# Scores of one tile of keys as two products a head, and several pieces of work moved earlier or later, in a macaron block on one core

## The chip, the cores and the metric

One NeuronCore of a Trainium2 chip runs the whole program. The metric is the device time of one execution in microseconds (us). Engines: TensorE (PE, with its weight loads PEld), VectorE (DVE), ScalarE (ACT), GpSimd (POOL) and SyncE (SP), which issues the DMAs.

## The reference

The block is half a feed-forward, attention, half a feed-forward, each with a layer norm ahead and a residual, on `x` of 2 x 512 rows and width 512. All is in fp32.

```python
x = x + 0.5 * ffn(layernorm(x))        # silu(a) * b @ down; a, b from scaled weights, 1792 wide
x = x + attn(layernorm(x))
x = x + 0.5 * ffn(layernorm(x))

# attn: 32 heads of 128 in 8 groups of G = 4 that share a key and a value head
q, k = rmsnorm(x @ Wq.T), rmsnorm(x @ Wk.T);  v = x @ Wv.T
scores = q @ k.T / sqrt(128)
bias = where(key > query, -1e30, slope[head] * (key - query))
out = softmax(scores + bias) @ v @ Wo.T
```

## The kernel before, in words

Every fp32 product is three products of split operands: a value is an upper part `_h` and a rest `_l` (the value less the upper part), and `matmul3` (lines 345 to 347) adds h*h, h*l and l*h in one PSUM bank. ScalarE makes most upper parts by a cast, VectorE or GpSimd the rests by a subtraction.

The feed-forward runs in steps of two chunks of the inner width, each with seven products in place of eight on mixed (added or subtracted) operands. In the first step `mix_lo(p, at)` (L1228 to L1235) makes the rests of the mixed tokens on VectorE, 1024 columns each.

The attention has 64 units n = 8 g + 4 b + t: group g of four heads, batch b, tile t of 128 queries. The attention is causal, so a unit with t has t + 1 tiles of 128 keys; t = 0 has one. The units are software-pipelined: the program is written out by hand for each engine as slots n = 0 to 63, and in slot n TensorE does

1. `scores(n)` (L574): per head three products of (t + 1) x 128 columns into a bank of its own, from `qT_h`, `qT_l` and `kT_h`, `kT_l`;
2. the values of unit n - 1 (`weigh_values`, L604 to L609, from `probT_h` and `probT_l`);
3. two of the seven products of a pair of projections of unit n + 4 (LEAD = 4; from group 2 on);
4. `turn_rows(n + 1)` (L565): transposes of the normalised rows of q and k;
5. `project_out(n - 1)`: four heads, each three products of 512 columns from `o_h`, `o_l` (the output weights) and `oT_h`, `oT_l`;
6. one or two more products of the seven, and the transposes of unit n's probabilities (L590).

Results go to eight PSUM banks. `result` takes the bank that was taken longest ago, and has TensorE wait (`evac`) until its last result was read. So an engine that reads a bank late holds up whatever takes that bank next.

VectorE in slot n: per head one custom operation (L1375) adds the bias to the scores and finds the maximum; then the inverse of the sums, `oT_l`, in even slots the sums of squares, `pair_roots(n + 2)` (L1348) and `add_products` (L1403 and L1411, which adds a product in PSUM to `rows`), then `turn_rows(n + 1)` (`qT_l`, `kT_l`, L1362 and L1367), the output's addition to `x_ring` (L1401) and `probT_l` (L1386). The roots of two units are `inverse_root` (L1090): eleven small steps on 10 columns, each waits for the one before; from the third on they read `row_root_y` and `row_root_a` or `row_root_b` from SBUF.

GpSimd in slot n (L1653): the squares of rows (L1645), `norm_rows(n + 2)` (L1651, waits for the roots), the rests of values, and per group of heads the rests of the next weights: `split_o` (`o_l`, four chunks of 512, in the second slot of a group) and `split_qkv` (`ahead_l` and `w_l_late`, 768 columns each; `QKV_WHEN` names the slots). ScalarE makes their upper parts and signals each.

Between the first feed-forward and the attention, `from_ffn_to_attention` does the projections of the first four units, `turn_normed` (transposes of normalised tokens) and `turn_rows(0)`.

Of the kernel before, what the change touches and what calls it, by code (L numbers as in the profile page):

```python
# [10 lines left out]
ALU = mybir.AluOpType  # L11
ACT = mybir.ActivationFunctionType
# [72 lines left out]
def build(nc, scaled, x_between, x, ffn_w, ffn_fac, ffn_fix, factor_lo, w_qkv, w_o, norm_w, out):  # L85
# [3 lines left out]
    with ExitStack() as ctx:  # L89
        def sb(name, shape, dt=F32, stack=ctx):  # L90
            return stack.enter_context(nc.sbuf_tensor(name, [P, *shape], dt))
# [112 lines left out]
        v_h, v_l = sb("v_h", [B, TB, HD], F32R), sb("v_l", [B, TB, HD], F32R)  # L204
        kT_h, kT_l = sb("kT_h", [S], F32R), sb("kT_l", [S], F32R)
        qT_h, qT_l = sb("qT_h", [G, P], F32R), sb("qT_l", [G, P], F32R)
# [100 lines left out]
        def qkv_place(g, block):  # L307
            at = QKV_BLOCKS[g][block]
            return qkv_h[at], qkv_l[at]

        def paired(n):
# [17 lines left out]
        def tensor_program():  # L329
# [184 lines left out]
            def from_ffn_to_attention():  # L514
                gate_up(0, STEPS - 1, 0, 1, (1,))
                gate_up(0, STEPS - 1, 1, 1)
                turn_normed(1, 0)
                down(0, STEPS - 1, 1)
                for n in range(LEAD):
                    project(n, "left")  # L520
                    project(n, "right")
                    if n == 1:
                        turn_normed(1, 1, (0, 1))
                turn_rows(0)
                turn_normed(1, 1, (2, 3))

# [47 lines left out]
            def scores(n):  # L574
                keys = (unit(n)[2] + 1) * P
                turned_q, turned_k = results["turn_q", n], results["turn_k", n]
                pe.wait_ge(evac[turned_q.bank], turned_q.nth)
                pe.wait_ge(evac[turned_k.bank], turned_k.nth)
                for h in range(G):
# [110 lines left out]
        def scalar_program():  # L690
# [187 lines left out]
            def from_ffn_to_attention():  # L878
                turn_normed(1, 0)
                for n in range(LEAD):  # L880
                    project_left(n)
                    project_right(n)
                    if n == 1:
                        turn_normed(1, 1, (0, 1))
                turn_rows(0)
                turn_normed(1, 1, (2, 3))

# [76 lines left out]
            def exponentials(n, heads):  # L964
                keys = (unit(n)[2] + 1) * P
                for h in heads:
                    r = results["scores", n, h]
                    act.wait_ge(evac[r.bank], r.nth)
# [42 lines left out]
            def slot(n):  # L1011
# [7 lines left out]
                if n:  # L1019
                    weigh_values(n - 1)  # L1020
                exponentials(n, range(soon, G))
                probabilities(n)
                ahead = n + LEAD
                if ahead < FIRST_PAIRED:
                    project_left(ahead)
                elif ahead < UNITS:
                    take_sum(ahead, 1) if n % 2 == 0 else take_sum(ahead - 1, 7)
                turn_rows(n + 1)
                if n % 2 == 0 and paired(n + 2):
# [49 lines left out]
        def vector_program():  # L1079
# [157 lines left out]
            def ffn_first(p):  # L1237
# [76 lines left out]
            def from_ffn_to_attention():  # L1314
# [14 lines left out]
                values_lo(2)  # L1329
                sum_squares(2)  # L1330
                values_lo(3)
# [3 lines left out]
                turn_normed(1, 1, (2, 3))  # L1335

# [32 lines left out]
            def scores(n):  # L1369
                g, _, i = unit(n)  # L1370
                keys = (i + 1) * P
                for h in range(G):
                    r = results["scores", n, h]
# [79 lines left out]
            def slot(n):  # L1453
# [21 lines left out]
                turn_rows(n + 1)  # L1475
                if ahead < FIRST_PAIRED:
# [41 lines left out]
        def pool_program():  # L1518
# [134 lines left out]
            def slot(n):  # L1653
                g, at = divmod(n, B * TB)
                if at == 1:
                    split_o(g, range(G))
                ahead = n + LEAD
                if n % 2 == 0 and paired(n + 2):
                    square_rows(n + 2)
                    square_rows(n + 3)  # L1660
                mixes_now = QKV_MIX_WHEN.get(at, ()) if SEVEN_FROM <= g + 1 < HKV else ()
                if at == 4:
                    mix_qkv(g + 1, *mixes_now)
                if n + 2 < UNITS:
                    norm_rows(n + 2)
# [8 lines left out]
                if at == 3:  # L1674
                    mix_qkv(g + 1, *mixes_now)
                if g < HKV - 1:
                    split_qkv(g + 1, *QKV_WHEN[g + 1 >= SEVEN_FROM].get(at, ()))
                if 0 <= n - LEAD - 1 < PAIRS:
# [288 lines left out]
```

## Time and profile before

| | us |
|---|---|
| median of 3 runs (lowest, highest) | 1238.32 (1237.34, 1238.6) |
| profiled execution | 1237.32 |
| its span | 1236.0 |
| granted TensorE clock | 1.00 |
| PE busy | 1215.9 (98%) |
| DVE busy | 827.4 (67%) |
| ACT busy | 756.6 (61%) |
| POOL busy | 649.1 (53%) |

The span is the time between the first and the last instruction of the profiled execution; what lies around it is 1.3 us. PE is the fullest engine by far. The duration of a matmul in the records is longer than the distance to the next one, since matmuls are pipelined: read starts, not durations, for what one costs. An instruction's idle time before it and what ended it stand in brackets behind its row.

### The profile page before, as it was taken

The page shows a single profiled execution, that of the slowest core. Times are in us where ns is not written, and L with a number is a line of the kernel's source. Part 1 is how long each engine was busy: PE and PEld are TensorE (multiplying, and loading weights), DVE is VectorE, ACT ScalarE, POOL GpSimd, SP SyncE. Part 2 cuts the span into 40 slices and gives each one's busy share as a digit, 9 for nine tenths or more (in the row PEclk, how much of TensorE's full clock was granted, in tenths as well). Part 3 has the DMA queues.
Part 4 walks back from the last instruction along what each step waited for, and adds up shares of the span by engine and source line. Part 5 has one row for each costly group of instructions (what it writes and reads, how often), then busy time and mean ns, then how long its engine had stood idle before and what let it go on. Part 6 is the DMA issues. An engine that isn't in the chain of part 4 may idle for free.

```text
span 1236.0 us, 18593 instructions
## 1 busy us (share of the span) xinstructions
PE 1215.9 (98%) x6418; PEld 1065.9 (86%) x6418; DVE 827.4 (67%) x2002; ACT 756.6 (61%) x1760; POOL 649.1 (53%) x526
## 2 busy tenths in 40 slices
PE   6999999999999999999999999999999999999999
PEld 5788888899998999999999999999999888888887
DVE  7966666676666667667677677667767778655555
ACT  4554442347677767767767767767767764544442
POOL 4696661734676624724824823823824343765550
PEclk9999999999999999999999999999999999999999
DMA  6142322212112122122122122122122010221101
GB/s 232 40 157 106 106 104 102 86 52 85 54 67 103 37 84 94 43 86 94 44 86 86 52 86 86 52 80 93 52 77 86 26 53 17 69 69 52 52 17 68
DMA packets 33453, 93.77 MB, mean 76 GB/s; under 512 B 4113, under 2 KB 4785, under 8 KB 31313
## 3 DMA queue, kind: packets, MB, share of 16 engines
q1 hardware_dynamic: 33120, 92.29, 21.8%
q8 instruction: 52, 0.85, 0.3%
q14 instruction: 41, 0.33, 0.1%
q10 hardware_dynamic: 240, 0.30, 0.1%
HBM read 62.69 MB, written 29.88 MB: 75 GB/s over the span
## 4 chain that ended last, share of the span: by engine, by line
PE 91%; DVE 4%; ACT 2%; POOL 1%; issue 1%; DMA 1%; SPq 0%; DVEq 0%; ACTq 0%; POOLq 0%
PE bank L345 21%; PE bank L347 21%; PE bank L346 21%; PE bank L590 5%; PE bank L424 4%; PE bank L430 4%; PE bank L425 4%; PE bank L604 3%; PE bank L609 3%; PE bank L605 3%; PE bank L569 2%; PE bank L373 1%; DVE stats L1106 1%; PE bank L572 1%; PE bank L361 0%
## 5 line engine op out<-in xcount | busy, mean ns | idle before, releaser
L1651 POOL TENSOR_TENSOR rows<-rows,row_root_y 128x640 f32<-128x640 f32 x64 | 80.6, 1260 | 205.1 <-DVE row_root_y L1102 205.1
L970 ACT ACTIVATE prob<-prob,neg_top 128x128 f32<-128x128 f32 (+3 forms) x256 | 141.2, 553 | 77.0 <-DVE neg_top L1375 76.4
L1645 POOL TENSOR_TENSOR square<-rows 128x640 f32<-128x640 f32 x64 | 79.2, 1254 | 161.0 <-DVE rows L1411 125.1
L1520 POOL TENSOR_TENSOR w_l_late<-raw_late,w_h_late 128x512 fp32r<-128x512 f32 (+1 forms) x59 | 90.5, 1548 | 74.9 <-ACT w_h_late L727 74.9
L979 ACT ACTIVATE prob<-prob,inverse 128x128 f32<-128x128 f32 (+3 forms) x256 | 123.0, 553 | 4.6 <-DVE inverse L1380 4.6
L1386 DVE TENSOR_TENSOR probT_l<-bank,probT_h 128x512 fp32r<-128x512 f32 x160 | 101.4, 683 | 21.8 <-ACT probT_h L985 21.7
L985 ACT CAST probT_h<-bank 128x512 fp32r<-128x512 f32 x160 | 84.6, 596 | 41.9 <-PE bank L590 41.9
L1375 DVE CUSTOM_DVE_ANT_0 prob<-bank,bias 128x128 f32<-128x128 f32 (+3 forms) x256 | 109.7, 484 | 0.0
L1168 DVE SCALAR_TENSOR_TENSOR x_rows<-bank,x_rows 128x512 f32<-128x512 f32 x112 | 75.7, 687 | 45.9 <-PE bank L430 45.9
L345 PE MATMUL bank<-o_h,oT_h 128*128 128x512 f32 x256 | 104.7, 409 | 0.0
L347 PE MATMUL bank<-o_h,oT_l 128*128 128x512 f32 x256 | 100.8, 394 | 0.0
L346 PE MATMUL bank<-o_l,oT_h 128*128 128x512 f32 x256 | 99.8, 390 | 0.0
L1411 DVE TENSOR_TENSOR rows<-bank,rows 128x384 f32<-128x384 f32 x72 | 40.0, 555 | 80.7 <-ACT rows L934 51.3
L345 PE MATMUL bank<-kT_h,qT_h 128*128 128x128 f32 (+3 forms) x256 | 86.5, 338 | 2.9 <-DVE qT_l L1362 2.9
L590 PE MATMUL bank<-ident,prob 128*128 128x128 f32 x640 | 81.4, 273 | 1.1 <-ACT prob L979 0.9
L347 PE MATMUL bank<-kT_h,qT_l 128*128 128x128 f32 (+3 forms) x256 | 82.2, 321 | 0.0
L346 PE MATMUL bank<-kT_l,qT_h 128*128 128x128 f32 (+3 forms) x256 | 82.1, 321 | 0.0
L590 PEld LDWEIGHTS bank<-ident,prob 128*128 128x128 f32 x640 | 73.8, 140 | 6.2 <-issue 1.7
L1520 POOL TENSOR_TENSOR w_l_early<-raw_early,w_h_early 128x512 fp32r<-128x512 f32 x37 | 49.6, 1357 | 41.9 <-ACT w_h_early L727 41.9
L1392 DVE TENSOR_TENSOR oT_l<-bank,oT_h 128x512 fp32r<-128x512 f32 x64 | 44.2, 690 | 30.9 <-ACT oT_h L990 30.9
L604 PE MATMUL bank<-probT_h,v_h 128*128 128x512 f32 x160 | 63.9, 399 | 0.3 <-ACT probT_h L985 0.3
L605 PE MATMUL bank<-probT_h,v_l 128*128 128x512 f32 x160 | 62.8, 392 | 0.0
(213 smaller groups left out, 3747.8 us busy)
## 6 DMA issues: line engine op xcount, KB each, us to landing
x_ring<-x_between SPq DMA_DIRECT2D x64, 256.0 KB, 2.6
x_between<-x_ring SPq DMA_DIRECT2D x56, 256.0 KB, 2.0
raw_late<-w_qkv SPq DMA_DIRECT2D x8, 1536.0 KB, 6.5
raw_early<-ffn_w SPq DMA_DIRECT2D x21, 512.0 KB, 4.0
scaled<-raw_early SPq DMA_DIRECT2D x21, 512.0 KB, 2.7
raw_late<-scaled SPq DMA_DIRECT2D x21, 512.0 KB, 3.7
raw_late<-w_o SPq DMA_DIRECT2D x8, 1024.0 KB, 5.0
x_between<-x_rows SPq DMA_DIRECT2D x8, 256.0 KB, 2.0
```

The source lines that it names most:

```text
L345: pe.matmul(bank, lh, rh, start=first, stop=False, skip_group_check=more)
L346: pe.matmul(bank, lh, rl, start=False, stop=False, skip_group_check=more)
L347: return pe.matmul(bank, ll, rh, start=False, stop=last, skip_group_check=more)
L590: last = pe.transpose(bank[:, h * P:(h + 1) * P], prob[:, h, j * P:(j + 1) * P], ident[:, :])
L604: pe.matmul(bank[:, :], v_h[:, b, j, :], turned[2 * j], start=j == 0, stop=False)
L605: pe.matmul(bank[:, :], v_l[:, b, j, :], turned[2 * j], start=False, stop=False)
L970: last = act.activation(p, p, ACT.Exp, bias=neg_top[:, h:h + 1], scale=-1.0, accum_out=total[:, h:h + 1])
L979: act.activation(p, p, ACT.Copy, scale=inverse[:, h:h + 1]).then_inc(prob_done, 1)
L985: act.copy(probT_h[:, j, :, :], banks[r.bank][:, :].rearrange("p (h q) -> p h q", h=G)).then_inc(probT_hi_done, 1)
L1375: dve.tensor_tensor_reduce(prob[:, h, 0:keys], banks[r.bank][:, 0:keys], bias[:, h, S - keys:S], -(2.0 ** -g), -MASKED, ALU.add, ALU.min, ...
L1386: dve.tensor_tensor(probT_l[:, j, :, :], banks[r.bank][:, :].rearrange("p (h q) -> p h q", h=G), probT_h[:, j, :, :].bitcast(F32), ALU.sub ...
L1520: return pool.tensor_tensor(lo, raw, hi.bitcast(F32), ALU.subtract)
```

## The change

It has six parts.

1. `in_halves(n)`: for the units with one tile of keys and n + 4 < 64 (n = 0, 4, ..., 56; fifteen of the sixteen) `kT_h` and `kT_l` lie side by side in one tile `kT`. Per head one product `qT_h` x [`kT_h` | `kT_l`] of 256 columns and one `qT_l` x `kT_h` of 128 stand in place of three of 128. Two heads share a bank. VectorE reads the second halves with two additions (rest + bias), waits for them, and then adds and reduces per head.
2. In those slots VectorE does `turn_rows(n + 1)` ahead of `pair_roots` and `add_products`.
3. GpSimd makes `o_l`'s first chunk in the first slot of a group of heads, ahead of `norm_rows`, and in the fifth slot the first block of `split_qkv` ahead of `norm_rows`.
4. `mix_lo(p, 2)` and `mix_lo(p, 3)` go from the end of `ffn_first` to `ffn_second`, one ahead of `down(p, 0, 1)` and one behind it.
5. The last `turn_normed` and `turn_rows(0)` stand ahead of the right half of project(3) on TensorE and ScalarE, and ahead of two later pieces on VectorE; in slot 0 ScalarE does `turn_rows(1)` ahead of the probabilities.
6. A dummy exponential in the transition and a dummy Silu ahead of the last values load ScalarE's tables earlier.

```diff
+        kT = sb("kT", [2, S], F32R)
+        kT_h, kT_l = kT[:, 0, :], kT[:, 1, :]
+        def in_halves(n):
+            return unit(n)[2] == 0 and n + LEAD < UNITS
@@ TensorE, from_ffn_to_attention (ScalarE alike)
                 for n in range(LEAD):
                     project(n, "left")
+                    if n == LEAD - 1:
+                        turn_normed(1, 1, (2, 3))
+                        turn_rows(0)
                     project(n, "right")
@@ TensorE, scores
+                if in_halves(n):
+                    for h in range(0, G, 2):
+                        r, bank = result("scores", n, h)
+                        for head in (h, h + 1):
+                            cols = (head - h) * 2 * P
+                            pe.matmul(bank[:, cols:cols + 2 * P], qT_h[:, head, :], kT[:, :, 0:P], start=True, stop=False, ...
+                            last = pe.matmul(bank[:, cols:cols + P], qT_l[:, head, :], kT_h[:, 0:P], start=False, stop=True, ...
+                        last.then_inc(full[r.bank], 1)
+                    return
@@ ScalarE
+                act.activation(total[:, 0:1], ident[:, 0:1], ACT.Exp)
...
+                if n == 0:
+                    turn_rows(n + 1)
                 probabilities(n)
...
+            act.activation(total[:, 0:1], ident[:, 0:1], ACT.Silu)
             weigh_values(UNITS - 1)
@@ VectorE
-                mix_lo(p, 2, 3)
...
                 product_lo(p, 1, 0, 0)
+                mix_lo(p, 2)
                 down(p, 0, 1)
+                mix_lo(p, 3)
@@ VectorE, scores
+                if in_halves(n):
+                    two = [results["scores", n, h] for h in range(0, G, 2)]
+                    for h, r in zip(range(0, G, 2), two):
+                        dve.wait_ge(full[r.bank], r.nth)
+                        rests = banks[r.bank][:, :].rearrange("p (h m c) -> p h m c", h=2, m=2)[:, :, 1, :]
+                        own_step(dve.tensor_tensor(prob[:, h:h + 2, 0:P], rests, bias[:, h:h + 2, S - P:S], ALU.add))
+                    for h in range(G):
+                        r = two[h // 2]
+                        if h == 0:
+                            own_wait()
+                        last = dve.tensor_tensor_reduce(prob[:, h, 0:P], banks[r.bank][...], prob[:, h, 0:P], ...)
+                        if h % 2:
+                            last.then_inc(evac[r.bank], 1)
+                    return
@@ VectorE, slot
-                if n % 2 == 0:
+                if in_halves(n):
+                    turn_rows(n + 1)
+                if n % 2 == 0 and n + LEAD - 2 < UNITS:
                     pair_roots(n + LEAD - 2)
                 if paired(ahead):
                     add_products(ahead, 2) if n % 2 == 0 else add_products(ahead - 1, 5)
-                turn_rows(n + 1)
+                if n + 1 < UNITS and not in_halves(n):
+                    turn_rows(n + 1)
@@ GpSimd, slot
                 if at == 1:
-                    split_o(g, range(G))
+                    split_o(g, range(1, G))
...
                 if at == 4:
                     mix_qkv(g + 1, *mixes_now)
+                    split_qkv(g + 1, *splits[:1])
+                    splits = splits[1:]
+                if at == 0:
+                    split_o(g, (0,))
                 if n + 2 < UNITS:
                     norm_rows(n + 2)
```

VectorE in a slot with one tile of keys (the same rows in each of them from the third on). `qT_l`, `kT_l` are the rests of the next unit's turned queries and keys, `row_root_*` the steps of the roots, `rows<-bank,rows` is `add_products`. Before:

```order
L1346 TENSOR_REDUCE sums<-square 128x5 x2
L1093 TENSOR_SCALAR row_root_m<-sums 128x10
L1095 TENSOR_SCALAR row_root_y<-row_root_m 128x10
L1098 SCALAR_TENSOR_TENSOR row_root_a<-row_root_y 128x10
...
L1102 SCALAR_TENSOR_TENSOR row_root_y<-row_root_b,row_root_y 128x10
L1411 TENSOR_TENSOR rows<-bank,rows 128x384
L1362 SCALAR_TENSOR_TENSOR qT_l<-bank,q_scale,qT_h 128x512
L1367 TENSOR_TENSOR kT_l<-bank,kT_h 128x128
```

and now (`kT` is both halves of the keys):

```order
L1376 TENSOR_REDUCE sums<-square 128x5 x2
L1392 SCALAR_TENSOR_TENSOR qT_l<-bank,q_scale,qT_h 128x512
L1397 TENSOR_TENSOR kT<-bank,kT 128x128
L1122 TENSOR_SCALAR row_root_m<-sums 128x10
L1124 TENSOR_SCALAR row_root_y<-row_root_m 128x10
L1127 SCALAR_TENSOR_TENSOR row_root_a<-row_root_y 128x10
...
L1131 SCALAR_TENSOR_TENSOR row_root_y<-row_root_b,row_root_y 128x10
L1456 TENSOR_TENSOR rows<-bank,rows 128x384
```

The two rests went from behind the eleven steps and the sum to ahead of them.

GpSimd in the fifth slot of a group, as it is in n = 20, 28, ..., 52. `ahead_l<-raw_late` is the moved rest, `rows<-rows,row_root_y` is `norm_rows`. Before:

```order
L1645 TENSOR_TENSOR square<-rows 128x640 x2
L1595 TENSOR_TENSOR xn<-raw_late,xn 128x768
L1651 TENSOR_TENSOR rows<-rows,row_root_y 128x640
L1520 TENSOR_TENSOR v_l<-rows,v_h 128x128 x2
L1520 TENSOR_TENSOR ahead_l<-raw_late,ahead_h 128x768
L1520 TENSOR_TENSOR ahead_l<-xn,ahead_h 128x768
```

and now:

```order
L1694 TENSOR_TENSOR square<-rows 128x640 x2
L1644 TENSOR_TENSOR xn<-raw_late,xn 128x768
L1569 TENSOR_TENSOR ahead_l<-raw_late,ahead_h 128x768
L1700 TENSOR_TENSOR rows<-rows,row_root_y 128x640
L1569 TENSOR_TENSOR v_l<-rows,v_h 128x128 x2
L1569 TENSOR_TENSOR ahead_l<-xn,ahead_h 128x768
```

The first rest stands ahead of the operation that waits for the roots, and no longer behind it.

TensorE in the change: product 2 of the unit ahead in slot 28, and the scores of unit 29 later in the same slot, with the semaphores that they wait for (`evac6` is the release of bank 6):

```order
L351 MATMUL bank<-w_h_late,xnT_hi 128x384 [waits evac6,qkv_lo]
L352 MATMUL bank<-w_l_late,xnT_hi 128x384
...
L351 MATMUL bank<-kT,qT_h 128x256 [waits evac4,evac2,evac7]
L352 MATMUL bank<-kT,qT_h 128x256
L353 MATMUL bank<-kT,qT_l 128x256
L351 MATMUL bank<-kT,qT_h 128x256 [waits evac1]
...
L351 MATMUL bank<-kT,qT_h 128x256 [waits evac6]
```

The third head of the scores takes the bank of product 2, which `add_products` of this slot reads.

## Rows read from the trace of the kernel before

**Rows 1.** The page: busy time by engine, and the chain's shares by engine.

```profile
PE 1215.9 (98%) x6418; PEld 1065.9 (86%) x6418; DVE 827.4 (67%) x2002; ACT 756.6 (61%) x1760; POOL 649.1 (53%) x526
...
PE 91%; DVE 4%; ACT 2%; POOL 1%; issue 1%; DMA 1%; SPq 0%; DVEq 0%; ACTq 0%; POOLq 0%
```

**Rows 2.** Waits of PE by releaser: us in total, times, longest us.

```profile
PE bank L345 <- DVE qT_l L1362: 2.9, 4, 1.0
...
PE bank L424 <- DVE silu L1185: 0.8, 1, 0.8
```

**Rows 3.** Timeline of PE, scores(28): start us, us, line, operation, tiles.

```profile
599.35 0.30 PE L345 MATMUL bank<-kT_h,qT_h 128*128 128x128 f32 x1
...
600.73 0.44 PE L604 MATMUL bank<-probT_h,v_h 128*128 128x512 f32 x1
```

**Rows 4.** Timeline of PE, scores(29).

```profile
610.38 0.36 PE L345 MATMUL bank<-kT_h,qT_h 128*128 128x256 f32 x1
...
611.17 0.28 PE L345 MATMUL bank<-kT_h,qT_h 128*128 128x256 f32 x1
...
611.89 0.40 PE L604 MATMUL bank<-probT_h,v_h 128*128 128x512 f32 x1
```

**Rows 5.** Timeline of DVE, slot 28.

```profile
606.53 0.17 DVE L1093 TENSOR_SCALAR row_root_m<-sums 128x10 f32<-128x10 f32 x1
...
608.67 0.55 DVE L1411 TENSOR_TENSOR rows<-bank,rows 128x384 f32<-128x384 f32 x1
609.14 0.74 DVE L1362 SCALAR_TENSOR_TENSOR qT_l<-bank,q_scale,qT_h 128x512 fp32r<-128x512 f32 x1
609.80 0.28 DVE L1367 TENSOR_TENSOR kT_l<-bank,kT_h 128x128 fp32r<-128x128 f32 x1
...
611.89 0.41 DVE L1375 CUSTOM_DVE_ANT_0 prob<-bank,bias 128x256 f32<-128x256 f32 x1
```

**Rows 6.** Timeline of ACT, slot 28.

```profile
606.29 0.69 ACT L958 ACTIVATE qT_h<-bank,q_scale 128x512 fp32r<-128x512 f32 x1 [0.43 <-PE bank L569]
...
607.41 0.84 ACT L899 CAST ahead_h<-raw_late 128x768 fp32r<-128x768 f32 x1
```

**Rows 7.** Timeline of POOL, slot 28.

```profile
608.84 1.26 POOL L1651 TENSOR_TENSOR rows<-rows,row_root_y 128x640 f32<-128x640 f32 x1 [4.76 <-DVE row_root_y L1102]
...
610.89 1.85 POOL L1520 TENSOR_TENSOR ahead_l<-raw_late,ahead_h 128x768 fp32r<-128x768 f32 x1
```

**Rows 8.** Timeline of DVE, slot 12.

```profile
416.96 1.01 DVE L1093 TENSOR_SCALAR row_root_m<-sums 128x10 f32<-128x10 f32 x1
```

**Rows 9.** Timeline of POOL, slot 12.

```profile
416.09 1.84 POOL L1520 TENSOR_TENSOR ahead_l<-xn,ahead_h 128x768 fp32r<-128x768 f32 x1
```

**Rows 10.** Timeline of DVE, the roots of the layer norm ahead of the attention.

```profile
253.64 1.12 DVE L1098 SCALAR_TENSOR_TENSOR ln_root_a<-ln_root_y 128x4 f32<-128x4 f32 x1
```

**Rows 11.** Timeline of POOL, the same moment.

```profile
253.49 1.25 POOL L1645 TENSOR_TENSOR square<-rows 128x640 f32<-128x640 f32 x1 [10.23 <-ACT rows L925]
```

**Rows 12.** Timeline of POOL, slots 8 and 9.

```profile
372.75 2.40 POOL L1520 TENSOR_TENSOR sum_l<-sum,sum_h 128x1024 fp32r<-128x1024 f32 x1
375.11 5.06 POOL L1520 TENSOR_TENSOR o_l<-raw_late,o_h 128x512 fp32r<-128x512 f32 x4
```

**Rows 13.** Timeline of ACT, slot 24, the first of a group of heads.

```profile
562.37 1.14 ACT L912 CAST o_h<-raw_late 128x512 fp32r<-128x512 f32 x2 [1.69 <-PE bank L347]
```

**Rows 14.** Timeline of PE, the third head of scores(25).

```profile
564.33 0.28 PE L345 MATMUL bank<-kT_h,qT_h 128*128 128x256 f32 x1
```

**Rows 15.** Timeline of ACT, slot 8.

```profile
373.92 1.14 ACT L912 CAST o_h<-raw_late 128x512 fp32r<-128x512 f32 x2 [1.34 <-PE bank L347]
```

**Rows 16.** Timeline of PE, the first head of project_out(8).

```profile
381.41 0.39 PE L345 MATMUL bank<-o_h,oT_h 128*128 128x512 f32 x1
```

**Rows 17.** Timeline of DVE, first feed-forward, second step's start.

```profile
50.72 5.23 DVE L1235 TENSOR_TENSOR mix_l<-mix,mix_h 128x1024 fp32r<-128x1024 f32 x2
```

**Rows 18.** Timeline of ACT, the evacuation behind the weights' splits.

```profile
64.98 1.20 ACT L759 COPY part<-bank 128x512 f32<-128x512 f32 x2
```

More of the change, by code:

```diff
@@ L204, in build @@
         v_h, v_l = sb("v_h", [B, TB, HD], F32R), sb("v_l", [B, TB, HD], F32R)
-        kT_h, kT_l = sb("kT_h", [S], F32R), sb("kT_l", [S], F32R)
+        kT = sb("kT", [2, S], F32R)
+        kT_h, kT_l = kT[:, 0, :], kT[:, 1, :]
         qT_h, qT_l = sb("qT_h", [G, P], F32R), sb("qT_l", [G, P], F32R)
@@ L523, in from_ffn_to_attention @@
                         turn_normed(1, 1, (0, 1))
-                turn_rows(0)
-                turn_normed(1, 1, (2, 3))
             def project(n, part):
@@ L578, in scores @@
                 pe.wait_ge(evac[turned_k.bank], turned_k.nth)
+                if in_halves(n):
[3 more added lines that the diff above has]
+                            cols = (head - h) * 2 * P
+                            pe.matmul(bank[:, cols:cols + 2 * P], qT_h[:, head, :], kT[:, :, 0:P], start=True, stop=False,
+                                      skip_group_check=True)
+                            last = pe.matmul(bank[:, cols:cols + P], qT_l[:, head, :], kT_h[:, 0:P], start=False, stop=True,
+                                             skip_group_check=True)
+                        last.then_inc(full[r.bank], 1)
+                    return
                 for h in range(G):
@@ L879, in from_ffn_to_attention @@
                 turn_normed(1, 0)
+                act.activation(total[:, 0:1], ident[:, 0:1], ACT.Exp)
                 for n in range(LEAD):
                     project_left(n)
+                    if n == LEAD - 1:
+                        turn_normed(1, 1, (2, 3))
+                        turn_rows(0)
                     project_right(n)
@@ L884, in from_ffn_to_attention @@
                         turn_normed(1, 1, (0, 1))
-                turn_rows(0)
-                turn_normed(1, 1, (2, 3))
             def split_qkv(g, *blocks):
@@ L966, in exponentials @@
                 for h in heads:
-                    r = results["scores", n, h]
+                    r = results["scores", n, h - h % 2 if in_halves(n) else h]
                     act.wait_ge(evac[r.bank], r.nth)
@@ L1027, in slot @@
                     take_sum(ahead, 1) if n % 2 == 0 else take_sum(ahead - 1, 7)
-                turn_rows(n + 1)
+                if n:
+                    turn_rows(n + 1)
                 if n % 2 == 0 and paired(n + 2):
@@ L1329, in from_ffn_to_attention @@
                 values_lo(2)
-                sum_squares(2)
-                values_lo(3)
+                turn_normed(1, 1, (2, 3))
                 dve.wait_ge(q_scale_done, 1 + HKV)
@@ L1334, in from_ffn_to_attention @@
                 turn_rows(0)
-                turn_normed(1, 1, (2, 3))
+                sum_squares(2)
+                values_lo(3)
             def values_lo(n):
@@ L1371, in scores @@
                 keys = (i + 1) * P
+                if in_halves(n):
[8 more added lines that the diff above has]
+                            own_wait()
+                        last = dve.tensor_tensor_reduce(prob[:, h, 0:P], banks[r.bank][:, h % 2 * 2 * P:h % 2 * 2 * P + P],
+                                                        prob[:, h, 0:P], -(2.0 ** -g), -MASKED, ALU.add, ALU.min, neg_top[:, h:h + 1])
+                        if h % 2:
+                            last.then_inc(evac[r.bank], 1)
+                    return
                 for h in range(G):
@@ L1474, in slot @@
                     add_products(ahead, 2) if n % 2 == 0 else add_products(ahead - 1, 5)
-                turn_rows(n + 1)
+                if n + 1 < UNITS and not in_halves(n):
+                    turn_rows(n + 1)
                 if ahead < FIRST_PAIRED:
@@ L1661, in slot @@
                 mixes_now = QKV_MIX_WHEN.get(at, ()) if SEVEN_FROM <= g + 1 < HKV else ()
+                splits = QKV_WHEN[g + 1 >= SEVEN_FROM].get(at, ()) if g < HKV - 1 else ()
                 if at == 4:
                     mix_qkv(g + 1, *mixes_now)
+                    split_qkv(g + 1, *splits[:1])
+                    splits = splits[1:]
+                if at == 0:
+                    split_o(g, (0,))
                 if n + 2 < UNITS:
@@ L1675, in slot @@
                     mix_qkv(g + 1, *mixes_now)
-                if g < HKV - 1:
-                    split_qkv(g + 1, *QKV_WHEN[g + 1 >= SEVEN_FROM].get(at, ()))
+                split_qkv(g + 1, *splits)
                 if 0 <= n - LEAD - 1 < PAIRS:
```

## Prediction

> **What bounds the kernel now.** I read the page first. The reader is to see that TensorE is busy 98% of the span and owns 91% of the chain that ended last [rows 1]. So only two things move the time: what TensorE issues, and where it waits. The waits by releaser come next. Inside the attention they are small: four waits for `qT_l`, 2.9 us together and 1.0 the longest, and one of 0.8 for a `silu` in the first half [rows 2]. There is little left to win by taking waits away, and every new wait of TensorE counts in full. The timelines of one unit and its neighbours then give durations, and, on VectorE and GpSimd, how much room each result has before TensorE asks for it. Times are in microseconds of the profiled run.
>
> **1. The scores of one tile of keys, 15 units (n = 0, 4, ..., 56).** Now twelve products of 128 columns go from 599.35 to the next line at 600.73: 1.38 for twelve, 0.115 each [rows 3]. Twelve of 256 columns go from 610.38 to 611.89: 1.51, and 0.12 each after the first of a stretch [rows 4]. The changed unit has four of 256 and four of 128 columns: 4 x 0.12 + 4 x 0.115 = 0.94. It saves 1.38 - 0.94 = 0.44, I take 0.43. Fifteen units would give 6.4; the first is counted under 4, so here 14 x 0.43 = -6.0. Width costs almost nothing between 128 and 256 columns, and that is all the gain. Bounds: 0.115 less if a 256-wide pair hides as well as a 128-wide one (-7.6), and 0.06 more for each if changing widths costs something (-2.7).
>
> The Trainium skill ("TensorE: Matmul & The Clock Gate", Back-to-back issue gap) gives for one isolated product a gap that grows with its columns over 2.4 GHz. By that rule 256 + 128 columns cost what 3 x 128 do, and this term would be about zero. The rows show otherwise (0.115 against 0.12), so the sum keeps -6.0.
>
> **2. VectorE and ScalarE in such a slot.** VectorE has two operations of 256 elements more; a 256-wide one holds it 0.41, paced 0.34 [rows 5], and the exponentials start up to 1.0 later. ScalarE still waits 0.43 for TensorE before `qT_h` at 606.29 [rows 6], so the delay ends there. Cost 0; bounds 0 and 0.4 a unit if that idle time were used up already.
>
> **3. The order on VectorE, and GpSimd's rests ahead.** This is where I expect the time to go. Before, in a slot with one tile of keys, VectorE takes the roots of two units (eleven small steps from 606.53, so 0.195 a step until `add_products` at 608.67, where the last overlaps it), then `qT_l` (0.66 by starts, until `kT_l` at 609.80) [rows 5]. GpSimd waits 4.76 for the last root, norms, and only at 610.89 begins the rest `ahead_l<-raw_late`, 1.85 long [rows 7], though ScalarE delivered its upper half at 607.41 + 0.84 = 608.25 [rows 6]. So the roots never meet a GpSimd operation.
>
> In the change, `qT_l` and `kT_l` come first. `qT_h` ends at 606.98, `qT_l` and `kT_l` (0.66 and 0.28) run from 607.0 to 607.9, and the roots begin at 607.95. GpSimd, however, no longer waits for the roots: it starts `ahead_l` at 608.3. The third step reads `row_root_y` twice.
>
> What happens to such steps beside GpSimd is in the trace. `row_root_m` took 1.01 in place of 0.17 from 416.96 on and ended at 417.97, while GpSimd's operation from 416.09 ended at 417.93; `ln_root_a` took 1.12 from 253.64 on and ended at 254.76, while the one from 253.49 ended at 254.74 [rows 8 to 11]. Both waited for GpSimd's end and then ran at once. In the second, GpSimd came in between two dependent steps.
>
> So the third step starts at 610.2, nine steps of 0.205 end at 612.05, and `add_products` (0.55) ends at 612.6, not 609.2. Who waits: product 2 of the unit ahead is in the bank that the third head of scores(n+1) takes. That head starts at 611.17 before [rows 4]; with the shorter scores it could at 610.75. It waits until 612.6: 1.85 lost, five units (20, 28, 36, 44, 52): +9.25. In n = 12 an old wait of 0.6 for `qT_l`, one of the four [rows 2], goes and some 2.2 come: +1.6.
>
> At the start of a group of heads (16, 24, ..., 56) the moved piece is the first `o_l` of four, 5.06 / 4 = 1.26 long [rows 12]. Its upper half is due half of 1.14 after 562.37, less the 0.4 that TensorE is earlier: about 562.6 [rows 13]. VectorE's roots, moved there as in the other slot, run from 561.2 to 563.3, so four or five steps stand behind it; they end at 564.7 and `add_products` at 565.2. The third head could start at 564.33 - 0.42 = 563.9 [rows 14]: 1.35, six units: +8.1. Bounds for the two places: without any meeting the roots end at 610.0 and the sum at 610.65, against 610.7: 0 to 0.1 a slot. With one more meeting, with the norm that follows, 1.2 each more.
>
> The Trainium skill ("SBUF — State Buffer", Who interferes with whom, and its Summary) says that GpSimd and a VectorE operation with two SBUF inputs share one port pair, and that the one that starts second fully blocks. This speaks against the change, and both meetings above agree with it. A sum that had no lock would be the first rival's.
>
> In n = 8 and 9 all four `o_l` came after one `sum_l` of 2.40 and ended at 380.17 [rows 12]. Now the first waits for ScalarE's `o_h` (373.92 + 0.57 [rows 15]) until 374.5, and norm, square and `sum_l` follow it (1.26 + 1.26 + 1.25 + 2.40), so the three others run from 380.6 to 384.4, some 0.3 less by the shorter scores; project_out(8) asks for its heads from 381.41 on, one each 0.68 [rows 16]. The last is asked for at 383.1 with the same shift: +1.0, bounds 0 and 1.5.
>
> **4. The first rows' turn.** The wait of 1.0 before scores(0) [rows 2] goes, and with it a table load before the first exponential, which the dummy one moves into idle time of ScalarE. But slot 0 has the longer way on VectorE of part 2, and the same meeting with `o_l`; the values of unit 0 then wait for `probT_l`. I take -0.25 with the first unit's halves; bounds -1.5 and +0.5.
>
> **5. The mixes.** `mix_l` x2 holds VectorE for 5.23 from 50.72, and TensorE waits 0.8 for the `silu` behind it [rows 2, 17]. One of them, 2.6, now lands behind `down`, ahead of the weights that ScalarE splits before it evacuates two banks from 64.98 on [rows 18], which TensorE takes again right behind. I take 0.3 of the 0.8 as kept; bounds 0 and 0.8. In the second feed-forward TensorE has no wait at this place. The dummy Silu: 0.
>
> **Sum.** -6.0 - 0.25 - 0.3 = -6.55; +9.25 + 1.6 + 8.1 + 1.0 = +19.95; together +13.4. The profiled run took 1237.32 (span 1236.0 and 1.3 around it); 1250.7 on that. The median shown is 1.0 above that run, so I forecast 1251.7. Its own range is 1245 to 1257: from a stall a third smaller at each of the eleven places (-6) to one more meeting at some (+5).
>
> **The rivals.**
> First, no meeting that matters: VectorE's chain of steps keeps GpSimd out, or the roots end before TensorE asks. Then -6.55 stands, the wait of 0.6 in n = 12 goes, +1.0 stays: about -6, 1232 (1229 to 1235). For it: the roots of the slot shown ran undisturbed (11 steps in 2.14 [rows 5]). Against: GpSimd sat idle by the wait for them then, and where it did not, they were held.
> Second, only one of the two kinds of slot meets (`o_h` comes late enough, or `ahead_l` early enough to end in time): -6 + 8 or 9, about 1240 to 1243, slightly slower. It depends on some 0.7 of timing at the start of a group.
> Third, the scores save nothing, because changing widths costs what the products save, and the meetings occur: 1251.7 + 6 = 1258. The 0.12 of the 256-wide products speaks against it.
>
> **How the numbers follow.** Forecast 0.65, first rival 0.24, second 0.09, third 0.02. The first ends faster, the second just above. The bound for a difference that can be told here is 0.2%, 2.5 us. Faster is the first rival with a little of the second less a little: 0.25. Same, 0.05, is a weak form of the second. Slower is the rest, 0.70. The range from 1231 to 1256.5 takes in the first rival's middle, for it alone holds more than 0.2.
>
> **What would show it.** In the profile after: products of a changed unit over 0.94 from first to next line (right for 1); in slots 20, 28, ... a `row_root_a` of 1.5 to 1.9 that ends with GpSimd's `ahead_l`, and in 16, 24, ... one of about 1 to 1.3 that ends with `o_l`; TensorE waiting at the third head of the next scores for VectorE's `rows` (line 1456), some 1.3 to 1.9 eleven times; no `qT_l` wait any more. The forecast is wrong if all `row_root` steps stay at 0.17, or if that third head never waits: then the time is 1232. It is half wrong if the waits are there but stand in only one kind of slot.

## The result, and the profile after

| | before | change |
|---|---|---|
| median, us | 1237.26 (1236.85 to 1238.6, 6 runs) | 1244.19 (1242.96 to 1245.36, 6 runs) |
| span of the profiled run, us | 1236.0 | 1242.8 |
| DVE busy, us | 827.4 | 852.5 |

The change is slower: 1.0052 of the time before, 95% interval 1.0041 to 1.0063, that is +6.9 us. Forecast were +13.4, and a time of 1251.7. The sign and the place were right, and the size was about half of the forecast.

The page after, busy time and chain by engine (compare [rows 1]):

```profile
PE 1213.7 (98%) x6358; PEld 1060.6 (85%) x6358; DVE 852.5 (69%) x2032; ACT 754.5 (61%) x1762; POOL 653.3 (53%) x526
...
PE 77%; DVE 13%; ACT 4%; POOL 2%; issue 2%; DMA 1%; SPq 0%; ACTq 0%; DVEq 0%; POOLq 0%
```

VectorE's share of the chain went from 4% to 13%. The waits of PE by releaser (us in total, times, longest) name it (compare [rows 2]):

```profile
PE bank L351 <- DVE rows L1456: 10.9, 12, 1.2
...
PE bank L351 <- DVE qT_l L1392: 1.4, 2, 0.8
...
PE bank L351 <- POOL o_l L1569: 0.5, 2, 0.3
```

A wait for `rows` didn't exist before. There are twelve, one in each even slot with one tile of keys from 12 to 56. Here is slot 28 of the change on VectorE, GpSimd and TensorE (answers to [rows 5], [rows 7], [rows 4]):

```profile
608.48 0.17 DVE L1122 TENSOR_SCALAR row_root_m<-sums 128x10 f32<-128x10 f32 x1
608.68 0.17 DVE L1124 TENSOR_SCALAR row_root_y<-row_root_m 128x10 int32<-128x10 int32 x1
608.89 0.17 DVE L1127 SCALAR_TENSOR_TENSOR row_root_a<-row_root_y 128x10 f32<-128x10 f32 x1
609.09 1.73 DVE L1129 TENSOR_TENSOR row_root_b<-row_root_a,row_root_m 128x10 f32<-128x10 f32 x1
610.86 0.17 DVE L1131 SCALAR_TENSOR_TENSOR row_root_y<-row_root_b,row_root_y 128x10 f32<-128x10 f32 x1
...
612.17 0.55 DVE L1456 TENSOR_TENSOR rows<-bank,rows 128x384 f32<-128x384 f32 x1
```

```profile
608.94 1.85 POOL L1569 TENSOR_TENSOR ahead_l<-raw_late,ahead_h 128x768 fp32r<-128x768 f32 x1 [4.19 <-ACT ahead_h L922]
612.33 1.26 POOL L1700 TENSOR_TENSOR rows<-rows,row_root_y 128x640 f32<-128x640 f32 x1 [1.54 <-DVE row_root_y L1131]
```

```profile
600.01 0.36 PE L593 MATMUL bank<-kT,qT_h 128*128 128x256 f32 x1
...
600.96 0.45 PE L624 MATMUL bank<-probT_h,v_h 128*128 128x512 f32 x1
...
611.29 0.28 PE L353 MATMUL bank<-kT,qT_l 128*128 128x256 f32 x1
612.77 0.39 PE L351 MATMUL bank<-kT,qT_h 128*128 128x256 f32 x1 [1.20 <-DVE rows L1456]
```

The reader is to see one chain. GpSimd starts at 608.94 and ends at 610.79. The step of 10 columns that starts on VectorE at 609.09 ends at 610.82, ten times its usual length. Seven steps follow, then the sum until 612.72, and TensorE's third head starts at 612.77 in place of 611.41. The scores themselves take 0.95 now (600.01 to 600.96), not 1.38. The third head starts 1.36 late; with 0.13 more in the products right behind it that is the 1.49 of the table below.

But for the scores and the first rows' turn TensorE runs the same order in both kernels, so the difference of their starts, unit by unit, splits the result (change less before, us; a slot is named by VectorE's work in it, and TensorE's loss then shows in the scores of the next unit):

| where | measured | forecast |
|---|---|---|
| start of the program (differs by run) | -0.3 | - |
| mixes, first feed-forward | -1.1 | -0.3 |
| first rows' turn until scores(0) | -1.1 | } -0.25 |
| unit 0 and slot 1 | +0.5 | } |
| two products a head, 14 units | -5.9 | -6.0 |
| slots 20, 28, ..., 52 (5 of 1.49) | +7.4 | +9.25 |
| slot 12 (+1.49, and -0.68 of an old wait) | +0.8 | +1.6 |
| slots 16, 24, ..., 56 (6 of 0.92) | +5.5 | +8.1 |
| slots 8 and 9 | +1.1 | +1.0 |
| slot 31 | +0.2 | - |
| sum at scores(60) | +7.1 | +13.4 |
| from there to the end | -0.3 | 0 |

### The profile page after: what moved, and what is told of

Its sections match the earlier page's. It is cut to its first block, busy times and chain, and to the rows that moved or that the text cites. A ratio compares the mean times of both kernels' runs of the same rounds, so it can differ in the third digit from the quotient of the medians.

```text
span 1242.8 us, 18505 instructions
## 1 busy us (share of the span) xinstructions
PE 1213.7 (98%) x6358; PEld 1060.6 (85%) x6358; DVE 852.5 (69%) x2032; ACT 754.5 (61%) x1762; POOL 653.3 (53%) x526
## 4 chain that ended last, share of the span: by engine, by line
PE 77%; DVE 13%; ACT 4%; POOL 2%; issue 2%; DMA 1%; SPq 0%; ACTq 0%; DVEq 0%; POOLq 0%
PE bank L351 18%; PE bank L353 18%; PE bank L352 18%; PE bank L436 4%; PE bank L430 4%; PE bank L431 4%; PE bank L610 3%; DVE probT_l L1431 3%; ACT prob L993 2%; PE bank L629 2%; PE bank L624 2%; PE bank L625 2%; DVE row_root_b L1129 2%; PE bank L576 2%; DVE sums L1376 1%
## 5 line engine op out<-in xcount | busy, mean ns | idle before, releaser
L1420 DVE CUSTOM_DVE_ANT_0 prob<-bank,bias 128x256 f32<-128x256 f32 (+3 forms) x196 | 96.0, 546 | 0.0
L351 PE MATMUL bank<-kT,qT_h 128*128 128x256 f32 (+3 forms) x196 | 71.0, 362 | 12.3 <-DVE rows L1456 10.9
L1569 POOL TENSOR_TENSOR o_l<-raw_late,o_h 128x512 fp32r<-128x512 f32 x32 | 40.6, 1292 | 63.0 <-ACT o_h L935 63.0
L353 PE MATMUL bank<-kT,qT_l 128*128 128x256 f32 (+3 forms) x196 | 65.7, 335 | 0.0
L352 PE MATMUL bank<-kT,qT_h 128*128 128x256 f32 (+3 forms) x196 | 65.7, 335 | 0.0
L1392 DVE SCALAR_TENSOR_TENSOR qT_l<-bank,q_scale,qT_h 128x512 fp32r<-128x512 f32 x64 | 47.9, 749 | 22.8 <-ACT qT_h L981 22.0
```

Source lines behind the costliest of these rows:

```text
L351: pe.matmul(bank, lh, rh, start=first, stop=False, skip_group_check=more)
L352: pe.matmul(bank, lh, rl, start=False, stop=False, skip_group_check=more)
L353: return pe.matmul(bank, ll, rh, start=False, stop=last, skip_group_check=more)
L1420: dve.tensor_tensor_reduce(prob[:, h, 0:keys], banks[r.bank][:, 0:keys], bias[:, h, S - keys:S], -(2.0 ** -g), -MASKED, ALU.add, ALU.min, ...
L1569: return pool.tensor_tensor(lo, raw, hi.bitcast(F32), ALU.subtract)
```

## The experiments

Ratios are to the runs of the kernel before on the same chip. "Lost" is what TensorE's starts fall behind in one slot beside the kernel before, the 0.42 of the scores apart.

**e1: both of GpSimd's moves back.**

```diff
-                    split_o(g, range(1, G))          # at == 1
+                    split_o(g, range(G))
-                    split_qkv(g + 1, *splits[:1])    # at == 4, ahead of norm_rows
-                    splits = splits[1:]
-                if at == 0:
-                    split_o(g, (0,))
```

> The change with both of GpSimd's moves taken back (the first o_l and the first ahead_l stand behind norm_rows again); all else as in the change. Theory (a GpSimd operation holds up VectorE's root steps, and TensorE waits for the sum behind them): no root step is longer than 0.2 us, the waits of TensorE for VectorE's rows at the third head of the next scores go, 6 x 1.49 + 6 x 0.92 + 1.1 (n = 8) = 15.5 us less than the change's 1244.2, and up to 1.2 of small waits left: 1229 to 1230, 0.6% faster than before. Rival (the waits come from VectorE's own order and its longer scores, GpSimd's rest only fills idle time): the waits stay, 1242 to 1244.

Measured: 1235.74, ratio 0.999 (0.9981 to 0.9999). All root steps of the attention are short but one (0.59 in slot 6, beside GpSimd's `sum`; the kernel before has one of 0.56 there), and no wait for `rows` is left, as both halves of the theory about the cause say. But the time fell by 8.5 and not by 15: TensorE now waits for the rests themselves, in the slot behind. Waits of e1, and TensorE in slot 29:

```profile
PE bank L351 <- POOL ahead_l L1569: 3.3, 5, 0.7
...
PE bank L351 <- POOL o_l L1569: 1.3, 6, 0.2
```

```profile
609.01 0.34 PE L353 MATMUL bank<-ahead_h,sum_l 128*128 128x384 f32 x1
610.02 0.45 PE L351 MATMUL bank<-ahead_h,sum_h 128*128 128x384 f32 x1 [0.67 <-POOL ahead_l L1569]
```

It loses 0.96 in five slots where the change loses 1.49, and 0.52 in six where the change loses 0.92. Counted from the start of scores(28), the roots begin 1.29 later than before (8.47 against 7.18): 0.87 of it are `qT_l` and `kT`, which now stand first, and 0.42 the longer way of the scores on VectorE. So `norm_rows` and all that stands behind it on GpSimd are later. GpSimd's moves took that wait away, and put a longer one in its place. I had priced only the wait that goes.

**e2 and e3: one move back each.** e2 undoes the `ahead_l` lines of the diff above, e3 the `o_l` lines.

> The change with only the move of ahead_l (fifth slot of a group) taken back; the first o_l still stands ahead of norm_rows. Theory: the six waits of about 1.4 in slots 12, 20, ..., 52 go, the six of 0.8 in slots 16, 24, ..., 56 and those of slot 8 stay: 1244.2 - 8.9 = 1235.3. Rival (VectorE's order alone): 1242 to 1244.

> The change with only the move of the first o_l taken back; ahead_l still stands ahead of norm_rows. Theory: the six waits of 0.8 in slots 16, 24, ..., 56 and those of slot 8 go, the six of 1.4 stay: 1244.2 - 5.5 - 1.1 = 1237.6. Rival (VectorE's order alone): 1242 to 1244.

Measured: 1240.92, ratio 1.0024 (1.0013 to 1.0035), and 1239.63, ratio 1.0018 (1.0009 to 1.0028). Each move brings the held root step and the wait for `rows` in its own slots and not in the other's, which speaks against VectorE's order alone. Each kernel is slower than expected, by e1's waits above all: e2 loses 0.96 in slots 20 to 52 where I had nothing, e3 0.5 in slots 16 to 56.

**e4: VectorE's order back, GpSimd's moves kept.**

```diff
-                if in_halves(n):
-                    turn_rows(n + 1)
-                if n + 1 < UNITS and not in_halves(n):
+                if n + 1 < UNITS:
                     turn_rows(n + 1)
```

> The change with VectorE's order taken back (pair_roots and add_products ahead of turn_rows again), GpSimd's moves kept. Theory: in the fifth slots the roots begin 0.9 earlier but GpSimd's ahead_l still meets them; qT_l and kT_l now stand behind it, so TensorE waits at the first head of the next scores, about 2.5 instead of 1.5, six times: +6; in the first slots the roots end before o_l starts, but qT_l comes some 0.5 late in place of the 0.9: -2.5. Sum about 1248 (1245 to 1251). Rival (the new order is what costs): 1237 or less.

Measured: 1248.58, ratio 1.0089 (1.0073 to 1.0104). As expected. GpSimd's `ahead_l` holds a root step in the fifth slots here too (slot 28: the fifth step, `row_root_y`, from 610.32, 1.72), and now `qT_l` stands behind it, which TensorE needs earlier, at the first head:

```profile
611.49 0.60 PE L610 MATMUL bank<-ident,prob 128*128 128x128 f32 x4
614.08 0.36 PE L351 MATMUL bank<-kT,qT_h 128*128 128x256 f32 x1 [2.00 <-DVE qT_l L1392]
```

So in the fifth slots GpSimd's move makes the meeting under either order of VectorE. In the first slots of a group no root step is held here: there it takes both. With GpSimd's moves kept, VectorE's new order loses less in the fifth slots (1.49 against 2.24) and more in the first (0.92 against 0.69). No run has VectorE's old order with GpSimd's pieces in their old place and the two products a head, so what the new order is worth by itself stays open.

**e5: GpSimd's pieces behind norm_rows, ahead of v_l.**

```diff
                     norm_rows(n + 2)
+                if at == 0:
+                    split_o(g, range(G))
+                if at == 4:
+                    split_qkv(g + 1, *splits[:1])
+                    splits = splits[1:]
                 if n % 2 == 0 and paired(n + 2):
                     values_lo(n + 2)
```

> The change, with GpSimd's two moved pieces in a third place: behind norm_rows (so behind the roots), but ahead of the rests of the values v_l (0.88 us for two). In the first slot of a group all four o_l, in the fifth the first ahead_l. Theory (the change traded the wait for a late rest against a longer wait behind a held-up root step; v_l is not urgent): no root step above 0.2, no wait for rows, and the rests come 0.9 earlier than with both moves taken back, where TensorE waited 0.84 and 0.4 for them; so those waits go too: 1235.7 - 5 x 0.95 - 0.13 - 6 x 0.52 = 1227.8, 0.8% faster than before. Rival (VectorE's later order itself makes the next wait, whatever GpSimd does): 1234 to 1236, with waits for rows or for v_l in the same slots.

Measured: 1234.37, ratio 0.9979 (0.997 to 0.9988): 6.6 more than expected. From slot 16 on it does what the theory says: it loses 0.13 and 0.03 a slot. But slots 1 and 9 lose 4.6 and 1.2. VectorE and GpSimd in slot 1:

```profile
281.13 0.82 DVE L1376 TENSOR_REDUCE sums<-square 128x5 f32<-128x640 f32 x1 [4.92 <-POOL square L1694]
281.87 0.68 DVE L1437 TENSOR_TENSOR oT_l<-bank,oT_h 128x512 fp32r<-128x512 f32 x1
```

```profile
274.86 5.03 POOL L1569 TENSOR_TENSOR o_l<-raw_late,o_h 128x512 fp32r<-128x512 f32 x4
279.84 1.25 POOL L1694 TENSOR_TENSOR square<-rows 128x640 f32<-128x640 f32 x1
```

In the first slots the squares of the unit ahead stand behind the four `o_l`, VectorE waits for them with `oT_l` in its queue, and TensorE 2.5 for that. I had named who waits for `v_l`, but not who waits for the squares. Another 1.7 of the 4.6 is TensorE's clock behind this wait: its products of 512 columns are up to 0.43 apart instead of 0.23, until 286.6. The window of e5:

```profile
282.70:287.00 4.30, 4.30 (x12) 3.34 (x13) 1.15 (x3) 3.21 (x9) 1.18 (x1) 0.60 0.58 249
```

The columns are length, PE, PEld, DVE, ACT and POOL busy, granted clock, DMA share and GB/s. The mean of 0.60 means that most of the stretch ran at 1.2 GHz.

**e6: half of the moved operation.** 384 of `ahead_l`'s 768 columns stay ahead of `norm_rows`, the others come right behind it.

```diff
-                    split_qkv(g + 1, *splits[:1])
+                        rest(l[:, 0:HALF], qkv_raw[block][:, 0:HALF], h[:, 0:HALF])
...
                     norm_rows(n + 2)
+                        rest(l[:, HALF:2 * HALF], qkv_raw[block][:, HALF:2 * HALF], ...).then_inc(qkv_lo, 1)
```

> The change with only the first 384 of the 768 columns of ahead_l ahead of norm_rows, the other 384 right behind it (o_l stays moved). Theory (a root step is held for exactly as long as GpSimd's operation runs): the long root step in slots 20, 28, ..., 52 falls from 1.73 to about 0.8, TensorE's loss there from 1.49 to about 0.6; 1244.2 - 6 x 0.9 = 1238.8. Rival (a fixed cost of any meeting, or the order of the queue and not the length): unchanged, 1243 to 1245.

Measured: 1239.56, ratio 1.0017 (1.0007 to 1.0026). The held step and GpSimd's operation in slot 28:

```profile
606.50 0.90 DVE L1129 TENSOR_TENSOR row_root_b<-row_root_a,row_root_m 128x10 f32<-128x10 f32 x1
```

```profile
606.35 1.03 POOL L1569 TENSOR_TENSOR ahead_l<-raw_late,ahead_h 128x384 fp32r<-128x384 f32 x1 [4.21 <-ACT ahead_h L922]
```

Operation 1.85 to 1.03, held step 1.73 to 0.90, TensorE's loss 1.49 to 0.69: microsecond for microsecond, so a fixed cost of any meeting is ruled out. A piece of `ahead_l` still stands ahead of `norm_rows`, as in the change, so the order as such is not the cost.

**e7 and e8: what kind of operation holds VectorE.** Both have GpSimd's moves undone and put an operation on scratch at the place.

```diff
+                        pool.wait_ge(qkv_hi, qkv_nth(g + 1, block) + 1)
+                        pool.wait_ge(sums_done, n + 4)
+                        pool.memset(square[:, :, :, :], 0.0)                                        # e7
+                        pool.tensor_tensor(square[:, 0, :, :], square[:, 1, :, :], square[:, 1, :, :], ALU.mult)   # e8
```

> Both of GpSimd's moves taken back; in the fifth slot of a group GpSimd fills a tile of 1280 columns that nobody needs at that time, at the place where the change has ahead_l (after the same wait for ScalarE). Theory A (only a GpSimd operation that reads SBUF holds VectorE's steps): every root step stays at 0.17. Theory B (any running GpSimd operation holds them): one root step in slots 20, 28, ... ends with the fill.

> As the run before, but GpSimd multiplies a tile of 640 columns with itself at that place, which nobody needs either. Both theories: one root step in slots 20, 28, ... is held until this operation of about 1.25 ends, so it shows 0.9 to 1.3; in the slots with no such operation all steps stay at 0.17. If no step is held, the length in the change comes from something that only ahead_l has (its other tiles).

In e8 one step is held in each of the six slots (slot 28: `row_root_b` from 606.26, 1.13, beside GpSimd's 606.11 + 1.25). In e7 the five slots from 20 on show no held step, though the fill runs amid them. GpSimd and VectorE, slot 28 of e7:

```profile
605.44 1.17 POOL L1717 MEMSET square<- 128x1280 f32 x1 [4.18 <-ACT ahead_h L922]
```

```profile
605.40 0.17 DVE L1127 SCALAR_TENSOR_TENSOR row_root_a<-row_root_y 128x10 f32<-128x10 f32 x1
605.60 0.17 DVE L1129 TENSOR_TENSOR row_root_b<-row_root_a,row_root_m 128x10 f32<-128x10 f32 x1
605.81 0.17 DVE L1131 SCALAR_TENSOR_TENSOR row_root_y<-row_root_b,row_root_y 128x10 f32<-128x10 f32 x1
```

In slot 12 of e7 the fill meets the first step instead, a `TENSOR_SCALAR` with one input, and that one is held to the fill's end (417.34):

```profile
416.17 1.17 POOL L1717 MEMSET square<- 128x1280 f32 x1
```

```profile
416.12 1.24 DVE L1122 TENSOR_SCALAR row_root_m<-sums 128x10 f32<-128x10 f32 x1
```

In e8 the step held in slot 12 is also one with one input (`row_root_y`, 1.14), as in the change (1.74). So theory A holds for steps with two inputs from SBUF and falls for this one. (Total times of e7 and e8, 1238.39 and 1241.2, are one run each, as are those of e11 and e12 below, 1235.85 and 1235.6.)

**e9: e5's order from the third group on.**

```diff
+                if at == 1 and g < 2:
+                    split_o(g, range(G))
...
+                if at == 0 and g >= 2:
+                    split_o(g, range(G))
```

> The last run's order (rests behind norm_rows and ahead of v_l), but for the first two groups of heads o_l stays where it was before the change, in the second slot: there the run e5 lost 4.6 us in unit 1 and 1.2 in unit 9. Theory: nothing else changes, 1234.4 - 4.4 - 1.2 = 1228.8, and up to 1.5 less where TensorE's clock doesn't fall near the end: 1227 to 1229, 0.7 to 0.8% faster than before. Rival (those losses are not from the place of o_l but from the order as a whole): 1233 to 1235.

Measured: 1230.21, ratio 0.9937 (0.9923 to 0.995), 6.8 us faster than before and 14 faster than the change. GpSimd in slot 28:

```profile
604.31 1.26 POOL L1700 TENSOR_TENSOR rows<-rows,row_root_y 128x640 f32<-128x640 f32 x1 [6.04 <-DVE row_root_y L1131]
605.52 1.85 POOL L1569 TENSOR_TENSOR ahead_l<-raw_late,ahead_h 128x768 fp32r<-128x768 f32 x1
607.34 0.87 POOL L1569 TENSOR_TENSOR v_l<-rows,v_h 128x128 fp32r<-128x128 f32 x2
```

The roots end before GpSimd starts, and TensorE takes `ahead_l` at 607.43, at once. The time is 1.4 above the sum of 1228.8. The profiled executions show 5.2 of the forecast 5.6 (spans 1234.1 and 1228.9), but e5's profiled one took 1235.51, 1.1 more than the median from which I had summed. In the profiled execution of e9, as in those of e5, e6, e7 and e10, TensorE's clock fell in the last slots. Windows of e9:

```profile
960.00:975.00 15.00, 14.73 (x91) 12.80 (x90) 11.82 (x38) 10.89 (x31) 3.52 (x3) 1.00 0.05 19
975.00:985.00 10.00, 8.36 (x37) 6.79 (x36) 8.30 (x25) 7.76 (x23) 4.74 (x6) 0.83 0.08 26
```

A mean of 0.83 means part of this stretch at 1.2 GHz; scores(63) then starts 1.5 later. All five lost 1.5 there, and the profiled executions of the change and the kernel before nothing, though they have the same two waits for the last units' `qT_l` (1.4 together, 0.8 the longest). It is not a trait of the kernel either: of e9's five executions, two had a mean granted clock of 1.000 (1227.6 and 1228.64) and three of 0.999 (1230.21 to 1230.3). What decides it stays open.

**e10: e9 with three products a head.** `in_halves` gives no unit for the computation, while the order stays.

> As e9 in every order, but the scores of one tile of keys as twelve products of 128 columns again, four banks and four custom operations of VectorE. Theory: each of 15 units costs TensorE 0.42 more, and VectorE's chain there is no bottleneck any more: 6.3 more than e9, 1234 to 1235. Rival (the two products a head only move TensorE's time into waits for the longer chain on VectorE and ScalarE): as e9 within 1.5 us, or less.

Measured: 1235.28, ratio 0.9985 (0.9976 to 0.9994): 5.1 more than e9. The gain of the two products is real. Small waits that e9 has and e10 has not (0.13 in six slots, 0.2 in slot 31) take 1 of the 6.3.

**e11: the mixes alone.** The diff is the mixes' three lines of the change.

> The kernel before with only the two mixes moved. As predicted (the weights' splits are late in place of the silu): the wait at 55 goes and some 0.6 come back at 62 to 66, so TensorE is 0.3 earlier at 90 us. As the change's trace reads: no wait comes back, TensorE is 0.9 to 1.1 earlier at 90 us, with nothing new in the second feed-forward.

TensorE starts 1.1 earlier at 90 us (after the difference at the start), and no wait comes back. VectorE, and GpSimd beside its last mix:

```profile
55.89 2.31 DVE L1235 TENSOR_TENSOR mix_l<-mix,mix_h 128x1024 fp32r<-128x1024 f32 x1
58.12 2.47 DVE L1168 SCALAR_TENSOR_TENSOR x_rows<-bank,x_rows 128x512 f32<-128x512 f32 x4
60.51 1.21 DVE L1235 TENSOR_TENSOR mix_l<-mix,mix_h 128x1024 fp32r<-128x1024 f32 x1
```

```profile
60.56 2.31 POOL L1521 TENSOR_TENSOR w_l_early<-mixed,w_h_early 128x512 fp32r<-128x512 f32 x1
```

Two mixes took 5.23 before [rows 17] and take 3.52 here. The last one is 1.21 long because it starts first, by 0.05: this time GpSimd's operation is the one that is held, 2.31 where it took 1.30 in the kernel before. I had moved 2.6 for each.

**e12: the first rows' turn alone.** The diff is part 5 of the change and the dummy exponential.

> The kernel before with only the first rows' turn moved (with the dummy exponential and ScalarE's slot 0). Theory: the wait of 1.17 before scores(0) goes, and scores(0) begins 1.1 earlier; without the longer scores on VectorE the next waits (for the probabilities of unit 0) stay at 0.7, so the gain is still about 1.0 at scores(4). As predicted: half of it and more is given back by then.

TensorE is 1.2 earlier at scores(0) and 1.1 at scores(4) (1.65 and 1.56, less 0.45 at 242 us that the start gives). As the theory says, nothing is given back. What the change loses in slot 1 (1.00) comes from `o_l` of slot 0 that holds a root step (273.58, 1.28), not from the turn: with `o_l` back in its place (e1, e3) slot 1 loses 0.24 and 0.22.

## Why the prediction was right in sign and twice too large

1. **Scores.** Right: 0.42 a unit, 14 units, and a cost that goes by streamed columns does not show here (0.95 for 256 + 128 four times, 1.38 for twelve of 128).
2. **Longer way on VectorE and ScalarE.** Right as to TensorE's next waits in the slot; e10 confirms it within 1 us. But the delay does not end at `qT_h` for everything: 0.42 of it reaches the roots, and is part of what e1's rests are late by.
3. **The meetings.** The mechanism, the places, the held lengths and who waits came as forecast: e6 shows the length's share by dose, e1 that VectorE's order alone does not make it, and e4 that GpSimd's move alone does in the fifth slots and does not in the first. The size was wrong, and this is the step that failed: "So the third step starts at 610.2, nine steps of 0.205 end at 612.05". Put on the change's times (scores(28) starts 0.66 later there), GpSimd started where I had it (608.94, forecast 608.3 + 0.66), but VectorE was 0.13 earlier, so that the third step got through. The fourth was held, and it ended together with GpSimd, 0.03 behind, where I had let the held step run afterwards. The rows that I read said so: `row_root_m` ended at 417.97 beside GpSimd's 417.93 [rows 8, 9], with none of its 0.17 on top. So seven steps stood behind the operation and not nine: 1.49 lost, not 1.85. In the first slots it was the same: I had four or five steps behind `o_l` (by my own times, 561.2 and 0.19 a step, seven had run at 562.6, so at most four were left), and the trace has the tenth held beside `o_l` (562.80 to 564.09) and one behind it, with 0.92 lost and not 1.35:

```profile
562.97 1.15 DVE L1129 TENSOR_TENSOR row_root_b<-row_root_a,row_root_m 128x10 f32<-128x10 f32 x1
564.15 0.17 DVE L1131 SCALAR_TENSOR_TENSOR row_root_y<-row_root_b,row_root_y 128x10 f32<-128x10 f32 x1
564.24 0.55 DVE L1456 TENSOR_TENSOR rows<-bank,rows 128x384 f32<-128x384 f32 x1
```

   Together with slot 12 (0.8 against 1.6) 5 x 0.36 + 6 x 0.43 + 0.8 = 5.2 of the 6.3 by which the sum was too large. Two readings behind this part were loose as well. `row_root_m` reads one tile, so of the two meetings that I read as those of steps with two SBUF inputs only `ln_root_a` is one. And two of my signs did not come: the held step is `row_root_b`, and waits for `qT_l` remain (two, in the last slots).
4. **First turn.** -0.6 against -0.25, in the bounds.
5. **Mixes.** -1.1 against -0.3, beyond the bound of 0.8. No wait came back, so the kept part is the whole wait and some more. I took for the moved instruction the duration that it had beside GpSimd (5.23 for two), though the meetings of part 3 say that this is not its own.
6. **The first rival** was wrong in its number as well. Without meetings I had 1232; e1 gives 1235.7, since a rest behind a later norm is itself waited for. 1230 takes a third order, e9's.

## What to carry to other kernels

A GpSimd operation with two SBUF inputs, moved into a gap, held the small VectorE step that started beside it until it ended, in each of the thirteen slots of the change where they met, though the step has only 10 columns. VectorE work with one operand in PSUM was not held: `probT_l<-bank,probT_h` took 0.68 or 0.69 all 160 times in the change, 24 of them wholly beside a 768-column rest on GpSimd. So lay GpSimd's work beside VectorE work on PSUM or behind such chains of small steps, and when a piece is late, look first for something non-urgent right ahead of it (here `v_l`) before moving it past a wait. When one chain is shortened to hide a wait, list what each queue has behind the moved piece in every phase of the loop: e5's first two groups lost 5.8 us, of which 2.5 is one wait behind a square and 1.7 the lower clock that followed. And never price a moved instruction by a duration that it had beside another engine's.

## What the runs showed of the hardware

A GpSimd fill of 1.17 us (no input) let VectorE's steps with two SBUF inputs pass at 0.17, while a GpSimd product of 1.25 held them for 1.13. A `TENSOR_SCALAR` of 10 columns with one input was held by the fill too (1.24). The Trainium skill ("SBUF — State Buffer", 🔬 SBUF: two separate sides) says that two SBUF inputs contend only with a GpSimd operation that reads SBUF, and that operations in a two-port mode contend with any. The five fills beside two-input steps agree, and the one beside the `TENSOR_SCALAR` agrees if that step runs in such a mode, which no row shows.

But not each GpSimd operation that reads SBUF held a step to its end. Ahead of the attention of the change, two of those with one SBUF input, and two of VectorE's steps beside them:

```profile
233.24 1.49 POOL L1799 TENSOR_SCALAR bias<-distance 128x512 f32<-128x512 int32 x1
234.81 1.49 POOL L1799 TENSOR_SCALAR bias<-distance 128x512 f32<-128x512 int32 x1
```

```profile
234.10 0.16 DVE L1129 TENSOR_TENSOR ln_root_b<-ln_root_a,ln_root_m 128x4 f32<-128x4 f32 x1
234.89 0.55 DVE L1131 SCALAR_TENSOR_TENSOR ln_root_y<-ln_root_b,ln_root_y 128x4 f32<-128x4 f32 x1
```

The step with two inputs at 234.10 passes at its usual length amid the first operation, and the one at 234.89, just behind the start of the second, takes 0.4 more and ends 0.87 ahead of it. The kernel before shows the same (236.25, 0.55). So the hold to the end is shown for GpSimd operations with two inputs, and for the fill beside a `TENSOR_SCALAR`.

The held step ends 0.02 to 0.04 behind GpSimd's end, in all slots of the change, e6 and e8: none of its own 0.17 comes on top.
